# A graph layer's edge loop: all 25 table rows of a chunk by indirect transfers instead of 21.4, the rest no longer by one-hot products on TensorE, and sign counts kept in a PSUM bank of their own

## What is computed

```python
h = jnp.maximum(_layernorm(x), 0.0)
xl = jnp.einsum('ni,nio->no', h, hetero_w[node_type]) + hetero_b[node_type]
ete = _lrelu(edge_type_emb[edge_type]); eae = _lrelu(edge_attr @ edge_attr_w)
x_i = xl[dst]; x_j = xl[src]
alpha = _lrelu(jnp.concatenate([x_i, x_j, ete, eae], axis=-1) @ att_w)
amax = jax.ops.segment_max(alpha, dst, num_segments=N)
alpha = jnp.exp(alpha - amax[dst])
denom = jax.ops.segment_sum(alpha, dst, num_segments=N)
alpha = alpha / (denom[dst] + 1e-16)
msg = jnp.concatenate([x_j, eae], axis=-1) @ lin_w * alpha
out = x + jax.ops.segment_sum(msg, dst, num_segments=N)
```

## Time and profile before

| | us |
|---|---|
| median of three runs (lowest, highest) | 5801.45 (5792.61, 5827.01) |
| the profiled execution, its own time | 5821.55 |
| its span, first to last instruction | 5819.7 |
| mean granted TensorE clock, as a share of full speed | 0.762 |

### The profile page before, as it was taken

One profiled execution on the slowest core, in us unless ns is written; L12 is line 12 of the kernel. 1 busy time (PEld: TensorE's weight loads), 2 busy tenths in 40 slices (PEclk: granted clock), 3 DMA queues, 4 the chain that ended last, 5 costly groups with the idle time before them and its releaser, 6 DMA issues.

```text
span 5819.7 us, 64841 instructions
## 1 busy us (share of the span) xinstructions
PE 3413.9 (59%) x21563; PEld 1921.9 (33%) x21563; DVE 2540.0 (44%) x6672; ACT 878.1 (15%) x2080; POOL 2783.2 (48%) x2793
## 2 busy tenths in 40 slices
PE   3456565665665565555666565666665666665660
PEld 2233333333333333333333333333333333333340
DVE  6343443443443444344444444444444444443464
ACT  2011111111111111111111111111111111111120
POOL 2554454454454444444554445455454454444417
PEclk7677777777787787777777777787777777777785
DMA  6111121121121121111211211211211211211112
GB/s 187 26 44 42 42 54 43 42 53 42 42 53 42 42 50 44 42 42 42 54 42 46 48 42 43 51 44 42 53 42 42 53 42 42 53 42 42 47 36 72
DMA packets 187871, 284.25 MB, mean 49 GB/s; under 512 B 74956, under 2 KB 142782, under 8 KB 186752
## 3 DMA queue, kind: packets, MB, share of 16 engines
q1 hardware_dynamic: 72864, 159.20, 9.5%
q0 software_dynamic: 90368, 55.56, 7.7%
q10 hardware_dynamic: 24288, 64.79, 3.1%
HBM read 207.03 MB, written 72.29 MB: 48 GB/s over the span
## 4 chain that ended last, share of the span: by engine, by line
another core or an unknown queue 37%; PE 29%; issue 17%; DVE 15%; POOL 2%; DMA 1%; DVEq 0%; SPq 0%; ACT 0%; POOLq 0%; ACTq 0%
PE ps_misc L678 21%; PE ps_pick L690 6%; DVE dst_f L1021 3%; DVE dscore L1055 2%; DVE sums L1148 2%; DVE gath L1048 1%; DVE node_buf L1083 1%; DVE h L1042 1%; POOL hib L515 1%; DVE onehot L1068 1%; PE ps_msg L722 1%; PE ps_attr L699 0%; DVE node_buf L1102 0%; PE ps_misc L645 0%
## 5 line engine op out<-in xcount | busy, mean ns | idle before, releaser
L481 POOL DMA_INDIRECT gath<-table_dram,meta x2675 | 2672.8, 999 | 2877.0 <-DMA meta<-meta_in 2003.3
L678 PE MATMUL ps_misc<-parts,dst_f 128*128 128x462 bf16 x9450 | 2345.3, 405 | 694.4 <-issue 615.4
L678 PEld LDWEIGHTS ps_misc<-parts,dst_f 128*128 128x128 bf16 x9450 | 988.7, 107 | 1921.5 <-issue 1187.0
L690 PE MATMUL ps_pick<-s_dst,onehot 122*128 122x128 bf16 x9375 | 736.5, 232 | 1402.7 <-DVE dscore L1055 895.8
L1055 DVE TENSOR_REDUCE dscore<-ps_pick 128x4 f32<-128x512 f32 x875 | 538.0, 629 | 1660.9 <-remote 1462.5
L690 PEld LDWEIGHTS ps_pick<-s_dst,onehot 122*128 122x128 bf16 x9375 | 609.2, 104 | 1559.0 <-DVE dscore L1055 948.5
L1042 DVE TENSOR_TENSOR h<-ps_misc,sel_mask 128x462 f32<-128x462 f32 x450 | 285.7, 635 | 1384.2 <-remote 1020.6
L575 ACT ACTIVATE wts<-args 128x50 f32<-128x50 f32 x125 | 30.7, 246 | 3484.4 <-DVE args L1126 2719.8
L588 ACT COPY rows<-sums 128x825 f32<-128x825 f32 x125 | 223.5, 1788 | 1080.6 <-DVE sums L1148 1080.6
L1021 DVE TENSOR_SCALAR dst_f<-dst_f,part_group 128x128 bf16<-128x128 f16 x1750 | 355.7, 284 | 0.9 <-DMA dst_f<-sel_code_dram 0.9
L1048 DVE TENSOR_REDUCE gath<-h 128x33 f32<-128x462 f32 x450 | 281.3, 625 | 2.7
(11 more groups left out here) (230 smaller groups left out, 1215.1 us busy)
## 6 DMA issues: line engine op xcount, KB each, us to landing
hib<-digit_dram SPq DMA_DIRECT2D x125, 612.5 KB
rows_dram<-rows ACTq DMA_DIRECT2D x125, 437.5 KB
gath<-table_dram,meta POOLq DMA_INDIRECT x2675
attr<-edge_attr_t_in SPq DMA_DIRECT2D x125, 200.0 KB
dst_f<-sel_code_dram SPq DMA_DIRECT2D x125, 128.0 KB
hib<-digit_dram SPq DMA_DIRECT2D x250, 50.0 KB
rows_dram<-gath ACTq DMA_DIRECT2D x1, 8575.0 KB, 46.8
hib<-digit_dram SPq DMA_DIRECT2D x250, 25.0 KB
```

The lines of the kernel that those rows point to most:

```text
L481: nc.gpsimd.indirect_dma_start(gath[u][:, t, :], None, table_dram, bass.IndirectOffsetOnAxis(ap=meta_sb[u][:, t:t + 1], axis=0)).then_inc( ...
L678: last = nc.tensor.matmul(ps_sel[:, j % 2, 0:VW * GN], sel_onehot[:, g, j * P:(j + 1) * P], parts[:, k, g, :], start=(g == 0 and k == 0), ...
L690: last = nc.tensor.matmul(ps_pick[:, g % 2, j * LO:(j + 1) * LO], onehot[0:KD, t * P:(t + 1) * P], s_dst[0:KD, k, :], start=(k == 0), stop ...
```

## The change

GpSimd gathers all 25 tiles of each chunk. The select codes with their transfers, the one-hots, the products and sums on VectorE, the 21 matmuls for each selected tile, the table's parts in SBUF and the set-up of all these are gone. `x_sb`, which shared memory with the parts, has memory of its own and isn't loaded again for the last stage. The sign counts accumulate in bank 0 of `ps_misc`, which the selects used: one matmul with zeros opens the sum, the five for each chunk add to it with neither start nor stop, another matmul with zeros closes it behind the last chunk, and VectorE reads it once.

```diff
-                    for t in range(T - TS[u]):
+                    for t in range(T):
                         nc.gpsimd.indirect_dma_start(
                             gath[u][:, t, :], None, table_dram,
                             bass.IndirectOffsetOnAxis(ap=meta_sb[u][:, t:t + 1], axis=0)).then_inc(gathered[u], 16)
...
-        ps_sel = ps_misc
-        ps_signs = ps_msg[:, 1, 2 * G * VW:2 * G * VW + NPP]
+        ps_signs = ps_misc[:, 0, 0:NPP]
...
                     load_hib(i * U + u, u)
-                    load_code(i * U + u, u)
                     load_attr(i * U + u, u)
...
                 dst_scores(c, 0)
                 dst_scores(c, 1)
-                if not final:
-                    select(*after, 0)
                 dst_scores(c, 2)
                 dst_scores(c, 3)
...
                 pe.wait_ge(msg_added, count(c))
-                pe.wait_ge(signs_summed, count(c + 1))
...
                 for g in range(4, PICKS):
                     dst_scores(c, g)
-                if not final:
-                    select(*after, 1)
-                    select(*after, 2)
 
                 pe.wait_ge(signs_ready, c + 1)
-                pe.wait_ge(msg_added, count(c + 1))
                 for t in range(BPC):
-                    last = nc.tensor.matmul(ps_signs, sign_hi[:, t, :], sign_lo[:, t, :], start=(t == 0),
-                                            stop=(t == BPC - 1))
+                    last = nc.tensor.matmul(ps_signs, sign_hi[:, t, :], sign_lo[:, t, :], start=False, stop=False)
                 last.then_inc(signs_mm, 1)
-                if not final:
-                    for j in range(3, TS[after[1]]):
-                        select(*after, j)
...
+            pe.wait_ge(unsorted_ready, 1)
+            nc.tensor.matmul(ps_signs, no_signs[:], no_signs[:, 0:NPP], start=True, stop=False)
             attr_product(0, 0)
-            pe.wait_ge(parts_ready, 1)
-            for j in range(TS[0]):
-                select(0, 0, j)
...
                 picks(c, 1)
-                sum_signs(c)
...
-                if not final:
-                    k_sel = select_others(*after)
-                    need(k_sel, at)
-                    take_product(*after, 0)
                 picks(c, 2)
-                if not final:
-                    take_sum(*after, 0)
-                    if not isinstance(i, int) or c + 2 < CHUNKS:
-                        select_first(i if u < U - 2 else i + 1, (u + 2) % U)
...
-                dve.wait_ge(gathered[u], (i + 1) * (16 * (T - TS[u])))
+                dve.wait_ge(gathered[u], (i + 1) * (16 * T))
```

More of the change, by code:

```diff
@@ L42 @@
 YW = F_IN + 2
-NG = 7
-GN = NPP // NG
 VW = F_IN + 1
@@ L670, in _ @@
             pe.wait_ge(diag_in, 3 * G * 16)
-            def select(i, u, j):
-                pe.wait_ge(sel_onehot_ready if j else sel_first_ready, i * U + u + 1)
-                pe.wait_ge(sel_read, count(selected(i, u) + (j - 1 if j > 1 else 0)))
-                for g in range(NG):
-                    for k in range(3):
-                        last = nc.tensor.matmul(ps_sel[:, j % 2, 0:VW * GN], sel_onehot[:, g, j * P:(j + 1) * P],
-                                                parts[:, k, g, :], start=(g == 0 and k == 0),
-                                                stop=(g == NG - 1 and k == 2))
-                last.then_inc(sel_mm, 1)
             def dst_scores(c, g):
@@ L749, in _ @@
                 chunk(ITERS - 1, u, u == U - 1)
+            nc.tensor.matmul(ps_signs, no_signs[:], no_signs[:, 0:NPP], start=False, stop=True).then_inc(
+                signs_summed, 1)
             pe.wait_ge(sign_parts_ready, 1)
@@ L782, in _ @@
             dve.sem_inc(tab_sb, 2)
-            start_at_one(dve, maskT_sb, eae_ready, signs_summed, picked, msg_added, sums_ready, sel_read)
+            start_at_one(dve, maskT_sb, eae_ready, picked, msg_added, sums_ready)
             steps = [0]
@@ L1150, in chunk @@
                                      ALU.add).then_inc(sums_ready, 1)
-                if not final:
-                    for j in range(3, TS[after[1]]):
-                        need(k_take, at)
-                        take_product(*after, j)
-                        k_take = take_sum(*after, j)
             dve.wait_ge(table_out, 16)
-            select_first(0, 0)
-            need(select_others(0, 0), 0)
             dst_onehot(0, 0)
-            for j in range(TS[0]):
-                take_product(0, 0, j)
-                need(take_sum(0, 0, j), 0)
-            select_first(0, 1)
             before = steps[0]
-            STEPS = U * 12 + TS_ITER
+            STEPS = U * 11
             with dve.Fori(0, ITERS - 1) as i:
@@ L1173, in _ @@
                 chunk(ITERS - 1, u, 0, u == U - 1)
-            sum_signs(CHUNKS)
-            dve.wait_ge(signs_summed, count(CHUNKS + 1))
+            dve.wait_ge(signs_summed, 1)
+            done(v.tensor_copy(sign_sums[:], ps_signs))
             done(v.tensor_copy(sign_parts[:, 0, :], sign_sums[:]))
```

137 lines of the change are left out of this document (11 added, 126 removed).

## The result

| | us |
|---|---|
| changed kernel, median of four runs (lowest, highest) | 5890.9 (5879.44, 5920.11) |
| kernel before, median of four runs (lowest, highest) | 5802.39 (5792.61, 5827.01) |
| ratio, 95% interval | 1.0154 [1.0105, 1.0202] |
| profiled execution of the changed kernel: own time, span, mean granted clock | 5889.51, 5887.7, 0.552 |

The change makes the kernel 1.5% slower here. The prediction said 7% faster; the time lies inside its range, the direction is wrong.

What follows compares the result with a forecast made beforehand. Bound by GpSimd's gather bursts plus gaps in which the other engines finish chunks. First bursts 272, one gap 18, 120 bursts 3780, 119 gaps 1071, tail 243: span 5384, at the median 5370 us; range 4850 to 5900.

Steps and rivals of the forecast that it cites:

- Bursts and gaps: In the loop, a chunk costs one GpSimd gather burst, about 27.3 us, plus one gap of 16.7 us finishing the chunk.
- the allowance counted in matmuls: Behind a gap of 20 us or more, TensorE gets about 85 to 100 matmuls away in a burst before it crawls.
- pairs of bursts that share one gap: After the change, one chunk ends under its burst, the next burst follows at once; near 60 waits of 18 us.
- remote: VectorE's idle time for a semaphore without a placeable sender, over 2400 us; forecast shorter per chunk and only ahead of picks.
- Two bursts then share one gap of 18 us, and I take 9 us a burst.: Gap after the change, between bursts in the loop: 9 us a burst, bounded by 0 and 16.7 us.
- 13.8 us as the last chunk: Term of the 18 us gap: the chunk done in it takes as long as the kernel's last chunk, 13.8 us.
- 11 matmuls done in the second burst by the crawl of the earlier trace: In a pair's second burst TensorE starts one matmul in 2.8 us, 11 in 31.5 us; about 3 us done before.
- Gathers back to back: Rival: with fewer matmuls GpSimd never waits in the loop; 4280 us at the median; chance 0.12.
- The slower side: Rival: smaller allowance, each burst needs its own gap of 15 us; 6075 us at the median; chance 0.2.
- The third rival: Gain and loss cancel in the loop, with mean gaps of 12 to 13 us: 5743 to 5860 us; chance 0.08.
- The 8.2 us that the selects cost where no gathers run: Behind the last gather, a chunk with selects was priced 8.2 us above the last chunk, which has none.
- Sign counts: Open sum in its own bank: TensorE drops two waits, the chunk's end on VectorE doesn't depend on it; nothing taken.

Runs made afterwards that it cites:

- e1: Changed kernel with each pick taking one of its three matmuls, 44 matmuls a chunk instead of 94: 5224.82 us where the kernel before takes 5752.15.
- g2: Changed kernel with 32 more small matmuls a chunk, read by nobody, ahead of pick group 4: 6201.43 us against 5789.6 for the kernel before.
- e2: Changed kernel with 1 gather a chunk instead of 25 from the sixth chunk on: 2716.41 us.
- e7: Kernel before, with SyncE released when the gathered rows are added, not when the sums are done, on a free chip: 4082.34 us, ratio 1.0002.
- f1: Changed kernel as it is, run on a free chip: 4420.86 us against 4090.46 for the kernel before, ratio 1.0808.
- g1: Changed kernel with each gather still indirect but taking rows 0 to 127 in order: 5919.01 us against 5789.6 for the kernel before, ratio 1.022.
- e4: Changed kernel with a plain GpSimd transfer of the same size in place of each gather: 2549.47 us.

## Why the prediction was wrong

**What held.** Bursts and gaps, the allowance counted in matmuls (e1, g2), pairs of bursts that share one gap, "remote" as the sign of it (all in the trace after), and that the engines' own work doesn't set the end. Burst: 31.5 us forecast; measured 3092.8 + 1031.2 - 97.1 us in 125 bursts, 32.2 us. That makes 0.7 x 120 = 84 us of the miss. The condition of failure that I named first, that the hold-back might go by time, is refuted by g2. The second, a lower clock in the gaps, came true (below).

**The step that failed: "Two bursts then share one gap of 18 us, and I take 9 us a burst."** The gap is 26.3 us. By its terms:

| term of the gap | forecast | measured (until 2564.06) |
|---|---|---|
| to recover behind the burst | 4.5 | 2.7 |
| the chunk | 13.8 | 20.9 |
| done before, in the second burst | -3 | 0 |
| scan's end to the gather | 2.7 | 2.7 |
| sum | 18 | 26.3 |

What failed above all is the term "13.8 us as the last chunk": the chunk in the gap takes 20.9 us. I priced it by the kernel's last chunk, noted as the one without selects. The 7.1 us between them are, as far as the runs tell:

- Some 2.6 us of work that the last chunk lacks: `attr_product` for the next chunk, which on TensorE stands ahead of the picks of groups 4 to 6, and VectorE's one-hot for the next chunk. e2 has both, and its quicker chunk takes 16.4 us (at a clock of 0.79, so a part of the 2.6 may be clock too).
- Some 2.9 us by TensorE's clock (below): the last chunk had run at 0.98.
- The other 1.6 us are at the chunk's start. VectorE waits 2.13 us ahead of `picks(c, 1)` (at 2543.35), which in e2 follows `picks(c, 0)` without a wait.

The 5 us by which the last chunk of the changed kernel is quicker than the two before it (14.3 against 19.3 and 19.0, with a wait of 2.15 us ahead of `picks(c, 4)` instead of 5.50) mix the first two, since it ran at the higher clock of the three.

The second term that failed, 11 matmuls done in the second burst by the crawl of the earlier trace rows, was none: the windows show x0.

With 12.7 us a burst instead of 9, 119 x 3.7 = 440 us more, and 84 us for the bursts, 5384 becomes 5908, against a span of 5887.7.

**TensorE's clock.** The granted clock fell from 0.762 to 0.552 in the mean, and reads 0.50 to 0.56 in the windows above, thus the level of 1.2 GHz for most of the time, after TensorE's busy share fell from 59% to 27%. One pick matmul takes 290 ns where the page of the kernel before has 232:

```profile
L690 PE MATMUL ps_pick<-s_dst,onehot 122*128 122x128 bf16 x9375 | 736.5, 232 | 1402.7 <-DVE dscore L1055 895.8
```

What it costs a chunk, e2 tells, in which no burst disturbs the chunks. The windows of two that follow each other, from scan to scan (columns as in the earlier trace rows):

```profile
1511.68:1528.05 16.37, 9.39 (x94) 7.97 (x94) 12.21 (x29) 6.52 (x16) 0.94 (x1) 0.79 0.30 90
1528.05:1547.31 19.26, 13.68 (x94) 12.04 (x94) 12.22 (x29) 6.53 (x16) 0.94 (x1) 0.52 0.25 77
```

The instructions are the same, 94 matmuls and 29 of VectorE, and VectorE's take the same time. At a granted clock of 0.79 the ten message matmuls take 1.56 us and VectorE waits 3.21 us ahead of `picks(c, 4)`; at 0.52 they take 2.96 us and it waits 5.50 us, the same two numbers as in the gap shown above. So the clock is 2.9 us of such a chunk. For the 51 long gaps that makes about 150 us, an estimate, which is more than the 88.5 us by which the kernel lost (5890.9 - 5802.39). No run has the changed kernel at the higher clock on a holding chip. By the estimate it would have come out about 1% faster, still far from 7%.

**The rivals.** "Gathers back to back" did come true on free chips, at 4421 us by measurement and 4280 by my sum; but there the kernel before, by its variant e7, has no gaps either. What I held against it, a shortage that nothing drains, is right on one kind of chip and wrong on the other. Here the Trainium skill (SBUF — State Buffer, Who interferes with whom) says that PE and ACT never wait on anyone and that DMA never contends with a compute engine. The rule speaks of SBUF's ports, and no run here shows that the hold-back comes from them. The holding chips disagree in effect, with 36.43 us ahead of a pick whose matmuls had run; the free chips agree. The slower side has the direction and, just, the time (5840 to 6075), by the wrong mechanism, one gap for each burst; only g2 looks like that, with 16.3 us a gap. The third rival, gain and loss cancelling at mean gaps of 12 to 13 us, has the measured 12.7; the time lies 31 us beyond its 5860, as the bursts were longer too. The 8.2 us that the selects cost where no gathers run were not to be had here: the gap fell by 4.0 only. Sign counts: nothing was forecast, and between nothing and 1.5% was found.

## What to carry to other kernels

Price a piece of a loop by a place where the same instructions run at the clock that they will have, and list what the last pass lacks: it is no sample of the others. Here TensorE's clock fell after it had lost half of its work, and by my estimate that made the difference between a small gain and the loss. When one engine's bursts stall the others, ask first what releases a burst, and move the release to the last read of the buffer; here that was worth 4 to 6% to the kernel before, where the exchange moved 1.5%. On a free chip it was worth nothing (e7). And run a rebalancing between engines on more than one chip: the change cost 1.5% on one kind and 8% on the other.

## What the runs showed of the hardware

- The same program took 5716 to 5802 us in four groups of runs and 4080 to 4090 us in two, each group on one chip. In the four, TensorE's completions reach the waiting engines late while GpSimd issues indirect transfers back to back (1.25 us each): VectorE stood idle up to 33.92 and 36.43 us in the pieces shown, and came back 2.7 to 4.0 us behind the last gather. In the burst behind a long gap, 77 (the windows after) to 100 matmuls start in all. What differs between the chips wasn't found. Each execution of the groups e to h has a span and a granted clock on record, that is, its instructions were recorded; whether the hold-back also comes in an execution that isn't recorded stays open.
- It goes by the count of matmuls, not by their time or their semaphores (g2), not by the rows gathered (g1), and it doesn't come with GpSimd's plain transfers, 552 ns apart (13.80 us for 25, e4), not even 200 of them without a pause.
- The same chunk of 94 matmuls takes 16.37 us at a granted clock of 0.79 and 19.26 at 0.52 (e2).
- On free chips a gather takes 1120 ns in the kernel with selects (e7) and 1023 ns in the one without (f1). What makes the difference was not tested.
